# Token stage: softmax scaling moved from TensorE and VectorE to GpSimd, a third buffer of probabilities, exponentials two tiles ahead

## The reference

```
# conv layer: plain attention with 32 features
xf = x.reshape(b, n, c)
theta, phi, g = xf @ W_theta + b_theta, xf @ W_phi + b_phi, xf @ W_g + b_g
x = x + (softmax(theta @ phi.T) @ g) @ W_out + b_out
# Nystrom attention with 8 heads of 32, 128 landmarks (means of 8 tokens)
q, k, v = heads(split(layernorm(x) @ w_qkv.T))
kernel_1 = softmax(q @ k_l.T)      # 1024 x 128 a head
kernel_2 = softmax(q_l @ k_l.T)    # 128 x 128
kernel_3 = softmax(q_l @ k.T)      # 128 x 1024
attn = kernel_1 @ (iterative_pinv(kernel_2) @ (kernel_3 @ v))
t = x + attn @ w_out.T + b_out
# top 2 of 16 experts
out = t + sum over the two experts of gate * (gelu(layernorm(t) @ W1[e]) @ W2[e])
```

## Time and profile before

| | us |
|---|---|
| median of 3 runs | 1000.76 |
| the runs | 999.50, 1000.76, 1002.37 |
| profiled execution | 999.48 |
| its span in the trace | 997.3 |
| TensorE busy | 908.4 |
| VectorE busy | 569.3 |
| ScalarE busy | 448.1 |
| GpSimd busy | 298.6 |

### The profile page before, as it was taken

The page is one execution under the profiler, slowest core; times in us unless marked ns, Lnnn a source line. Parts: engine busy times, 40 slices in busy tenths (PEclk is TensorE's granted clock), DMA queues, the critical chain, the costliest instruction groups (busy, mean ns, idle before and its releaser), DMA issues.

```text
span 997.3 us, 21748 instructions
## 1 busy us (share of the span) xinstructions
PE 908.4 (91%) x6980; PEld 699.0 (70%) x6982; DVE 569.3 (57%) x1585; ACT 448.1 (45%) x1004; POOL 298.6 (30%) x343
## 2 busy tenths in 40 slices
PE   5999989899999899999899999546899999999997
PEld 3565767565767565767556767335789999999996
DVE  3478857587857687866678866693222222222221
ACT  1424367433359443349443348253334444444442
POOL 3050001060001050001130000103467666767664
PEclk9699999899999999999899999857999999999999
DMA  3100000300000300000200000499444444444341
GB/s 106 43 2 1 1 2 23 107 1 1 2 1 2 126 3 1 2 1 2 86 1 1 1 2 2 135 252 326 125 67 71 66 69 66 69 65 64 62 65 16
DMA packets 47848, 50.76 MB, mean 51 GB/s; under 512 B 11073, under 2 KB 41153, under 8 KB 47777
## 3 DMA queue, kind: packets, MB, share of 16 engines
q0 software_dynamic: 15168, 18.85, 11.7%
q1 hardware_dynamic: 32608, 30.99, 10.3%
HBM read 33.00 MB, written 18.78 MB: 52 GB/s over the span
## 4 chain that ended last, share of the span: by engine, by line
PE 73%; DVE 13%; issue 5%; DMA 4%; ACT 3%; SPq 1%; POOL 1%; POOLq 0%; DVEq 0%; ACTq 0%
PE PS L982 12%; PE PS L530 11%; PE PS L991 11%; PE PS L851 7%; PE PS L559 6%; PE PS L622 4%; PE PS L723 3%; PE PS L633 3%; PE PS L704 3%; DVE neg_max L1206 3%; DMA out_dram<-low,row_of 3%; PE PS L627 3%; PE PS L709 2%; ACT arena L1053 1%; PE PS L718 1%
## 5 line engine op out<-in xcount | busy, mean ns | idle before, releaser
L391 POOL TENSOR_SCALAR aggr<-aggr 128x1 f32<-128x1 f32 x64 | 14.3, 223 | 519.6 <-DVE aggr L1326 519.6
L1206 DVE TENSOR_REDUCE neg_max<-PS 128x1 f32<-128x1024 f32 (+1 forms) x96 | 117.5, 1224 | 78.2 <-PE PS L633 27.4
L530 PE MATMUL PS<-ident,arena 128*128 128x128 f32 x1008 | 140.3, 287 | 19.8 <-DMA arena<-in_x_dram 6.9
L982 PEld LDWEIGHTS PS<-low 128*128 128x128 f32 x1264 | 155.1, 194 | 4.1
L530 PEld LDWEIGHTS PS<-ident,arena 128*128 128x128 f32 x1008 | 122.7, 150 | 46.9 <-issue 37.7
L982 PE MATMUL PS<-low 128*128 128x128 f32 x1264 | 155.3, 277 | 0.0
L991 PE MATMUL PS<-arena,low 128*128 x632 | 151.9, 384 | 3.3 <-issue 1.6
L439 POOL DMA_INDIRECT out_dram<-low,row_of x79 | 125.4, 1588 | 87.0 <-DVE low L1660 38.6
L1061 ACT COPY arena<-PS 128x1024 f32<-128x1024 f32 x96 | 98.4, 1025 | 92.0 <-PE PS L530 92.0
L991 PEld LDWEIGHTS PS<-arena,low 128*128 128x128 f32 x632 | 114.9, 192 | 18.0 <-issue 5.4
L1149 ACT ACTIVATE low<-PS 128x512 f32<-128x512 f32 x79 | 47.2, 597 | 156.6 <-PE PS L982 156.6
(11 more groups left out here) (203 smaller groups left out, 1312.2 us busy)
## 6 DMA issues: line engine op xcount, KB each, us to landing
arena<-in_L_ffn_W_dram SPq DMA_DIRECT2D x32, 512.0 KB, 5.7
arena<-in_x_dram SPq DMA_DIRECT2D x4, 1024.0 KB, 6.4
out_dram<-t SPq DMA_DIRECT2D x4, 1024.0 KB, 6.8
rows_scratch<-arena SPq DMA_DIRECT2D x4, 512.0 KB, 3.7
rows_scratch<-arena SPq DMA_DIRECT2D x8, 256.0 KB, 2.6
low<-rows_scratch,token_of POOLq DMA_INDIRECT x79, 2.9
out_dram<-low,row_of POOLq DMA_INDIRECT x79, 3.8
arena<-in_L_attn_w_qkv_dram SPq DMA_DIRECT2D x1, 768.0 KB, 4.8
```

The costliest lines, as they stand in the source:

```text
L530: mm = pe.transpose(PS[0:s.shape[1], dst_bank, n * P:n * P + s.shape[0]], s, ident[0:s.shape[0], 0:s.shape[0]])
L982: mm = pe.matmul(PS[:, 2 + p, hc * P:(hc + 1) * P], w1_now[:, p, c * H + hc * P:c * H + (hc + 1) * P], xgT[:, p, c, :], start=c == 0, stop ...
L1206: dve.tensor_reduce(dst, src, AX.X, ALU.max, negate=True).then_inc(s_max, 1)
```

## The change

- The inverses of the sums are no longer turned on TensorE. `turn_inverses`, `inverses_turned`, `inv_T` and their semaphores are gone.
- GpSimd gets `scale_probs(t)`: it waits for the inverses of tile t and multiplies the tile's probabilities by them in place, 128x1024 by 128x8 spread over the landmarks. The transposes of tile t wait for that (`scaled`) instead of for the exponentials. `out_t` becomes a plain copy.
- GpSimd does `scale_probs` of t first and then `deviation` of t - 3.
- A third buffer of probabilities, `third_probs`: the tiles use it and the two halves of `Pm` in turn. ScalarE does the exponentials of s + 2 ahead of the copy of tile s, instead of those of s + 1.
- On TensorE `turn_probs` of tile s moves from the start of a step to its end, behind `values` and `finish`.
- On VectorE `rows1` and `norm1` move ahead of the statistics, the statistics are split in `stats1` (ahead of `maxima`) and `moments1` (behind it).

```diff
@@ buffers
-        inv_T = arena[:, 30208:30720].rearrange("p (b d) -> p b d", b=2)
+        probs_of = lambda u: Pm[:, u % 2, :] if u < 2 * NT else (third_probs[:], Pm[:, 0, :], Pm[:, 1, :])[(u - 2 * NT) % 3]
+        third_probs = sb("third_probs", [P, N])
@@ GpSimd
-                for t in range(NT):
-                    pool.wait_ge(x2_done, i * NT + t + 1)
-                    apart(pool, "pool")
-                    deviation(t, i).then_inc(dev2_ready, 1)
+                def scale_probs(t):
+
+                    pool.wait_ge(inv_ready, i * NT + t + 1)
+                    mine = probs_of(2 * NT + t).rearrange("p (h m) -> p h m", m=M)
+                    pool.tensor_tensor(mine, mine, head_inv[:, t % 2, :].unsqueeze(2).broadcast_to([P, HEADS, M]),
+                                       ALU.mult).then_inc(scaled, 1)
+
+                for t in range(NT + 3):
+                    if t < NT:
+                        scale_probs(t)
+                    if t >= 3:
+                        pool.wait_ge(x2_done, i * NT + t - 3 + 1)
+                        apart(pool, "pool")
+                        deviation(t - 3, i).then_inc(dev2_ready, 1)
@@ TensorE
                     if k == 0:
-                        pe.wait_ge(s_exp, i * UNITS + u + 1)
+                        if u < 2 * NT:
+                            pe.wait_ge(s_exp, i * UNITS + u + 1)
+                        else:
+                            pe.wait_ge(scaled, i * NT + u - 2 * NT + 1)
...
-                    if s < NT:
-                        for k in range(2):
-                            turn_probs(2 * NT + s, k)
                     for k in range(2):
                         if s + 2 < NT:
                             scores(2 * NT + s + 2, k)
                     if s == 0:
                         queries(3)
+                    if s == 1:
                         pe.wait_ge(y_head_ready, i + 1)
-                    if s == 1:
                         pe.wait_ge(q_ready, i * 4 + 4)
                     if 1 <= s <= NT:
                         values(2 * NT + s - 1)
-                    if s < NT:
-                        turn_inverses(s)
                     if s >= 2:
                         finish(2 * NT + s - 2)
+                    if s < NT:
+                        for k in range(2):
+                            turn_probs(2 * NT + s, k)
@@ ScalarE
-                    if u >= 2:
+                    if u >= 2 * NT + 1:
+
+                        act.wait_ge(t_mm, i * UNITS + u - 2)
+                    elif 2 <= u < 2 * NT:
                         act.wait_ge(t_mm, i * UNITS + u - 1)
...
+                exponentials(2 * NT + 1)
+                query_rows(2)
                 for s in range(NT):
-                    if s + 1 < NT:
-                        exponentials(2 * NT + s + 1)
-                    if s == 0:
-                        query_rows(2)
+                    if s + 2 < NT:
+                        exponentials(2 * NT + s + 2)
                     turned(2 * NT + s)
@@ VectorE
-                        dve.tensor_tensor(OT[:, u % 2, :], PS[:, 0, 256:512], inv_T[:, u % 2, :], ALU.mult).then_inc(ot_ready, 1)
+                        dve.tensor_copy(OT[:, u % 2, :], PS[:, 0, 256:512]).then_inc(ot_ready, 1)
...
+                    if s >= 3:
+                        rows1(s - 3)
+                    if s >= 4:
+                        norm1(s - 4)
...
                     if s >= 3:
-                        rows1(s - 3)
-                    if s >= 4:
-                        norm1(s - 4)
+                        stats1(s - 3)
                     if s + 2 < NT:
                         maxima(2 * NT + s + 2)
+                    if s >= 3:
+                        moments1(s - 3)
                     if 1 <= s < NT:
                         out_t(2 * NT + s - 1)
-                    if s < NT:
-                        inverses_turned(s)
```

More of the change, by code:

```diff
@@ L253, in conv_attn_nystrom_moe_kernel @@
         inv_ready = sem("inv_ready")
[L254 to L255 removed]
+        scaled = sem("scaled")
         y_head_mm = sem("y_head_mm")
@@ L262, in conv_attn_nystrom_moe_kernel @@
         x2_done = sem("x2_done")
+        x2_stats = sem("x2_stats")
         dev_ready = sem("dev_ready")
@@ L666, in turn_probs @@
                     if k == 0:
-                        pe.wait_ge(s_exp, i * UNITS + u + 1)
+                        if u < 2 * NT:
+                            pe.wait_ge(s_exp, i * UNITS + u + 1)
+                        else:
+                            pe.wait_ge(scaled, i * NT + u - 2 * NT + 1)
                         if u >= 1:
                             copied(u - 1)
-                    mm = transposes(pe, 2 + k, [Pm[:, u % 2, (4 * k + n) * P:(4 * k + n + 1) * P] for n in range(4)])
+                    mm = transposes(pe, 2 + k, [probs_of(u)[:, (4 * k + n) * P:(4 * k + n + 1) * P] for n in range(4)])
                     if k == 1:
                         mm.then_inc(t_mm, 1)
[L674 to L685, removed]
                 def values(u):
@@ L1350, in rows0, with stats1, moments1 @@
                     moments(x1[:, t, :], t, x1_done)
+                def stats1(t):
+                    dve.wait_ge(pr_used, i * UNITS + 2 * NT + t + 1)
+                    dve.bn_stats(stats[:, 0:6], t2_row(t)).then_inc(x2_stats, 1)
+                def moments1(t):
+                    dve.wait_ge(x2_stats, i * NT + t + 1)
+                    dve.bn_aggr(aggr[:, t, 0:2], stats[:, 0:6]).then_inc(x2_done, 1)
                 def rows1(t):
@@ L1358, in rows1 @@
                     dve.tensor_tensor(t2_row(t), PS[:, 1, 0:D], x1[:, t, :], ALU.add).then_inc(pr_used, 1)
-                    dve.wait_ge(pr_used, i * UNITS + u + 1)
-                    apart(dve, "dve")
-                    moments(t2_row(t), t, x2_done)
                 maxima(1)
@@ L1498, in _ @@
                         inverses(s)
+                    if s >= 3:
+                        rows1(s - 3)
+                    if s >= 4:
+                        norm1(s - 4)
                     if s == 0:
+                        inverses(0)
                         dve.wait_ge(y_head_mm, i + 1)
@@ L1502, in _ @@
                                           scale_c.unsqueeze(2).broadcast_to([P, HEADS, HD]), ALU.mult).then_inc(y_head_ready, 1)
-                        inverses(0)
                     if s == NT - 1 and more:
@@ L1524, in _ @@
                     phi_out(i + 1, 1)
+                stats1(NT - 1)
                 norm1(NT - 2)
+                moments1(NT - 1)
                 if more:
```

14 lines of the change are left out of this document (3 added, 11 removed).

## The result

The changed kernel took 1016.39 us in the median (1013.72 to 1017.72, 4 runs), the kernel before 1000.13 us beside it: a ratio of 1.018, 95% interval 1.015 to 1.021. The profiled execution has a span of 1015.9 us against 997.3. The forecast was 1022, in a range of 1009 to 1033: slower, as forecast, but by 16 us in the medians (18.6 in the spans) instead of 22. The profiled execution, 1017.72 us, is the longest of the four, so its stretches at a lower clock may be more than the median one has.

The account below looks back on a forecast made before the run. TensorE was taken to bound a token step at 4.01 us, ScalarE right behind. Ring and tail +10.4, held normalisations +5.6 and clock +6.2 make +22.2 on 999.48: 1021.7, said as 1022, range 1009 to 1033.

Parts of the forecast that it names:

- its freed 17.6 us: TensorE's small products of L683 in the token stage go, 0.55 us a tile over 32 tiles, but not on the path.
- 0.27 x 5 = 1.35: Most a sample's token stage could gain, in us: steps of ScalarE's 3.74 instead of 4.01 for tiles 1 to 5.
- The ring: Token stage cycle of copy, values, finish, transposes, scores, maxima, exponentials, copy: 8.74 us for two tiles.
- the hold: VectorE's normalisations of tiles 0 to 3 held till 0.15 us behind GpSimd's product, 2.40 instead of 0.38: +5.6 us.
- The tail's chain: Once no scores are left, each tile is transposes, copy, values, finish and hand-offs in a chain: 3.67 us.
- One of the signs: TensorE waits 1.4 to 1.7 us at tiles 0, 1, 3 and 4 and 2.7 at tile 5, each sample.
- Ring and tail: Token stages end later, by 2.0 us in three samples and 4.4 in the last: +10.4 us.
- The clock: TensorE's granted clock falls after two of four long waits, 3.1 us each: 6.2 us, bounds 0 and 12.4.
- Rival 1: VectorE's normalisations are not held by this form of GpSimd product, or fall outside it: 1010 to 1016 us; chance 0.17.
- Rival 2: ScalarE's queue is never kept waiting, so a token step costs 3.74 us instead of 4.01: 994 us; chance 0.10.
- Rival 3: Ring and savings cancel in the token stage, so the change is neutral: 998 to 1004 us; chance 0.05.
- Rival 4: The clock falls at the middle waits too, two or three times a sample: 1044 us; chance 0.08.

Follow-up runs that it names:

- Run 6: The kernel before without the turned inverses and their copy on VectorE, the scaling left out of the computation: 997.12 us, ratio 0.9975.
- run 1: The changed kernel with the normalisations of tiles 0 to 3 moved to the end of VectorE's step: 1013.84 us, ratio to before 1.014.
- Run 3: The changed kernel with TensorE's step starting with the scores of s+3, and maxima and inverses a tile earlier on VectorE: 1005.65 us, ratio 1.004.
- run 7: The changed kernel with sixteen unused transposes of the identity on TensorE ahead of tile 5's values: 1014.63 us, ratio 1.016.
- run 5: The changed kernel with scores and maxima earlier, normalisations late, transposes directly behind the scores, and GpSimd's deviation of t-4 instead of t-3: 999.2 us, ratio 0.999.
- run 8: The changed kernel with scores early, normalisations late, transposes directly behind scores, and the head of the token stage reordered: 984.87 us, ratio 0.985.
- run 9: The kernel before with tile 2's scores ahead of the third query projection and their maxima ahead of the product of the head values: 999.48 us, ratio 0.999.
- run 2: The changed kernel without GpSimd's product and the waits for it, the scaling left out of the computation: 1013.65 us, ratio 1.014.
- run 4: The changed kernel with scores a tile earlier and the normalisations of tiles 0 to 3 behind the copy of the values: 1003.35 us, ratio 1.002.

## Why the prediction came out as it did

**TensorE is the bound, and its freed 17.6 us are off the path: right.** Run 6 shows them to be worth 1.43 us in the one stage in which the clock did not fall, against the 0.27 x 5 = 1.35 that the prediction gave as the most.

**The ring: right in mechanism and nearly in size.** The prediction had 8.74 us for two tiles; without holds tiles 2 and 4 of run 1 stand 8.81 apart. Counted from the first head values (291.34 before), the forecast of tiles 1 to 7 without the hold reads 12.3, 16.0, 21.1, 24.8, 29.9, 33.6, 37.2. Run 1 has 12.30, 16.55, 21.11, 25.36, 29.92, 33.60, 37.28 in its second sample. Tiles 2 and 4 are 0.6 off, since the 8.8 us are shared out more evenly between two tiles than in the walk; the rest is within 0.1. The tail's chain was 3.67 a tile and is 3.68. Run 3 opens the ring and 2.4 us a sample vanish. One of the signs named with it did not come: the walk put waits of 1.4 to 1.7 us at tiles 0, 1, 3 and 4 and 2.7 at tile 5, and the trace has 1.86, 0.92, 0.93, 0.98 and 2.05, with another 0.60 at tile 2.

**Ring and tail were put at 10.4 and are 11.3**: 48.29 - 45.87 = 2.42 three times, and 44.22 - 40.18 = 4.04. The forecast had 2.0 and 4.4.

**The step that failed in size: the hold, 5.6 forecast, 1.8 found** (48.74 - 48.29 = 0.45 three times, 44.64 - 44.22 = 0.42). Both numbers in it were off to the same side. GpSimd's product takes 1.90, not 2.35, and lies under the lower bound of 2.26, though the bounds were set by the same operation. The neighbours had two full operands and this one reads eight numbers over and over; whether that is the reason was not tried. With it the held normalisation takes 1.82, not 2.40. And VectorE's idle time is 1.06 in the new order, not 0.61. ScalarE's waits for the maxima, put at some 1.4, are at most 0.81 in the second sample behind the head of the stage. The sign and the place were right: each of tiles 0 to 3 is held, and ends 0.15 behind the product, as the row at 63.49 had it. All 16 of the profiled execution ended so, after 0.78 to 1.98 us; the 16 normalisations of tokens that met no product took 0.40 to 0.42. L1347, with an input in PSUM, is not held anywhere in the trace of before: its 32 operations took 0.482 to 0.485 us, 12 of them beside a GpSimd operation. But the statistics L1324, which read SBUF alone, were not held either: in the first stage they took 0.427 to 0.429 beside such an operation and without one. What makes the normalisation wait, and what decides which operation is held, no run shows.

**The clock: 6.2 forecast, 3.95 found** (1.36 + 1.24 + 1.35). The count was near, three falls in place of two, though two was no more than a choice between none and four: of the four longest waits, those ahead of tile 5, two were followed by a fall, and a third fall stood behind a 1.86 us wait ahead of tile 0, which the forecast had not counted. The price was wrong: 3.1 us was read off a fall at the change of samples, where 6.8 us run at half the clock and TensorE is the bound; the falls in the stage last 3.4 us and part of what they slow lies ahead of a wait. In sample 3 the wait behind the fall was gone and the next one grew.

Sum: 11.3 + 1.8 + 3.95 = 17.05, against 17.03 measured in the four stages. That it closes is no test of its own, since the terms are differences between these stages and those of runs 1 and 7; what tests them is that run 1 removes the hold, run 3 the ring, and that run 7's stages agree with one another. The remaining 1.5 us of the 18.6 between the spans lie ahead of and behind them.

**The rivals.** Rival 1 (no hold) would have had 1010 to 1016 and came close in time, for the wrong reason: the holds are in the rows. Rival 2 (ScalarE never waits) named the right next bound: runs 5 and 8 get there once the ring is open, which it was not. Rival 3 (ring and savings cancel) is out with it: it needed the ring near two old steps, and 8.81 stands above 8.02. Rival 4 is out: three falls behind the 24 waits of over 0.5 us ahead of values.

## What to carry to other kernels

When a step moves off the bounding engine, follow each buffer and each queue once around before counting the saving: a piece that is put behind two others in one queue can close a ring that no engine's busy time shows. Test the two apart, the added work by taking it out and the order by shifting it alone; here the added product cost 0.45 us a sample and the order 2.4. The gain appears only when the order gives the freed engine work to do from the start of the stage on.

## What the runs showed of the hardware that was not expected

- In the token stages and at the changes of samples the clock's falls began during waits of 1.8 to 2.1 us or up to 2 us behind them, but not one for one, and the length of the wait does not decide it. At the changes of samples half the clock came in 7 of 9 cases of 1.79 us (before, runs 6 and 9) and in 22 of 24 of 1.97 us (changed kernel, runs 1 to 5, 7 and 8). Inside the stage it followed 1.85 or 1.86 us in 1 of 16 cases (changed kernel, runs 1, 2 and 7), 1.99 us in none of 8 (runs 1 and 2), 2.01 us in 1 of 12 (runs 3 to 5), 2.05 us in 2 of 4 (changed kernel), 1.96 us in 3 of 4 (run 6). With 0.29 us of wait or less left at a change of samples it never did, in three profiled executions with three changes each. Where a fall inside the stage was followed by a change of samples 18 us later (sample 2 of the changed kernel) the latter had none; what decides this the runs do not show.
- A piece of TensorE's work has no fixed price. The values took 0.46 to 0.47 us start to start ahead of L683 and 0.57 ahead of the finish; finish ahead of transposes 0.96 to 0.97, ahead of scores 1.06. Taking eight small products out of the step saved 4.01 - 3.72 = 0.29 us in the order of run 5, not their 0.55. Why is not shown; what changes is the shape of the tiles from one piece to the next.
- GpSimd's product of 128x1024 with eight factors spread over it took 1.895 to 1.899 us in all 32 cases, less than half of the 4.519 us that 128x2048 with two full operands takes. Whether it is the operand or the length was not tried apart.
